# A fused attention and expert layer on one core: a new order at the step's border, and work moved from VectorE to GpSimd

## The reference

```python
q, k, v = x @ wq + bq, x @ wk + bk, x @ wv + bv        # 16 heads of 8
q, k = rope(q), rope(k)
scores = q k^T / sqrt(8), masked above the diagonal
x = layernorm(x + softmax(scores) v @ wo + bo)
probs = softmax(x @ wg)                                # 8 experts, top 1
location = number of earlier tokens (of all 16 sequences) with the same expert
keep a token if location < 512
x = layernorm(x + keep * gate * (x @ W[expert]^T + b[expert]))
```

## Time and profile before

| | |
|---|---|
| median of three runs | 492.28 us |
| the profiled execution: its time, its span | 493.83 us, 492.2 us |
| TensorE busy, weight loads busy | 85%, 74% of the span |
| VectorE, ScalarE, GpSimd busy | 70%, 34%, 34% |
| mean granted TensorE clock | 0.948 |
| instructions | 10410 |

### The profile page before, as it was taken

How to read it: one execution, slowest core, us unless ns; L and a number is a source line. 1 busy time by engine, 2 the same in 40 slices (tenths; PEclk the granted TensorE clock), 3 DMA queues, 4 the chain that set the end, 5 groups by cost and what they waited for, 6 DMA issues and landing times.

```text
span 492.2 us, 10410 instructions
## 1 busy us (share of the span) xinstructions
PE 418.6 (85%) x3270; PEld 362.4 (74%) x3270; DVE 345.4 (70%) x910; ACT 169.0 (34%) x370; POOL 165.2 (34%) x288
## 2 busy tenths in 40 slices
PE   2527398999999999999999999999999999989551
PEld 2425287979788888888888878787879787868441
DVE  7677346678787877788787878778777786844542
ACT  4404134333342424243333434333434342424100
POOL 5423202131424242433424251525252523231232
PEclk9997588999999999999999999999999999999856
DMA  4163977939385856777585849393939393310000
GB/s 119 48 102 90 150 137 107 140 87 137 74 147 86 144 79 135 91 126 97 121 104 121 106 105 126 90 135 82 149 83 140 84 141 65 30 31 1 11 1 21
DMA packets 145443, 47.29 MB, mean 96 GB/s; under 512 B 104317, under 2 KB 141697, under 8 KB 145418
## 3 DMA queue, kind: packets, MB, share of 16 engines
q1 hardware_dynamic: 141194, 43.30, 55.0%
q10 hardware_dynamic: 3456, 1.57, 1.8%
q0 software_dynamic: 768, 2.10, 1.5%
HBM read 30.70 MB, written 14.68 MB: 92 GB/s over the span
## 4 chain that ended last, share of the span: by engine, by line
PE 65%; DVE 17%; issue 6%; ACT 5%; SPq 2%; DMA 2%; POOL 1%; ACTq 1%; DVEq 0%; POOLq 0%
PE ps_pv L853 27%; PE ps_m L774 6%; PE ps_b L820 5%; PE ps_m L775 5%; PE ps_m L776 5%; DVE y_sel L616 4%; PE ps_a L830 4%; PE ps_m L794 3%; PE ps_b L805 2%; ACT probs L473 2%; PE ps_a L805 2%; PE ps_n L861 2%; DMA k_diag<-plain_parts 1%; SPq L314 1%; PE ps_n L901 1%
## 5 line engine op out<-in xcount | busy, mean ns | idle before, releaser
L853 PE MATMUL ps_pv<-probs,v_diag 128*128 128x64 f32 (+3 forms) x1024 | 191.1, 322 | 6.1 <-ACT probs L473 6.1
L853 PEld LDWEIGHTS ps_pv<-probs,v_diag 128*128 128x128 f32 x1024 | 150.3, 193 | 16.1 <-ACT probs L473 9.1
L473 ACT ACTIVATE probs<-ps_b 128x512 f32<-128x512 f32 (+1 forms) x176 | 96.9, 559 | 141.3 <-PE ps_b L805 140.5
L631 DVE TENSOR_REDUCE row_max<-ps_a 128x2 f32<-128x512 f32 (+3 forms) x176 | 109.8, 634 | 36.7 <-PE ps_a L805 36.4
L830 PE MATMUL ps_a<-k_plain,q_diag 128*128 128x64 bf16 (+3 forms) x512 | 66.3, 242 | 12.9 <-DMA q_diag<-plain_parts 7.2
L820 PE MATMUL ps_b<-q_plain,k_diag 128*128 128x64 bf16 (+3 forms) x512 | 65.9, 237 | 2.1 <-DMA k_diag<-plain_parts 2.1
L616 DVE TENSOR_REDUCE y_sel<-ps_m 128x128 f32<-128x1024 f32 x32 | 39.2, 1225 | 38.0 <-PE ps_m L794 37.3
L830 PEld LDWEIGHTS ps_a<-k_plain,q_diag 128*128 128x128 bf16 x512 | 35.3, 102 | 23.4 <-DVE row_max L631 13.0
L820 PEld LDWEIGHTS ps_b<-q_plain,k_diag 128*128 128x128 bf16 x512 | 37.6, 99 | 10.2 <-DMA k_diag<-plain_parts 2.4
L413 POOL COPY v_diag<-v_rows 64x128 f32<-64x128 f32 x64 | 18.6, 291 | 78.2 <-ACT v_rows L487 76.2
L805 PE MATMUL ps_a<-mask_a_bf,ident_bf 128*128 128x128 bf16 (+2 forms) x176 | 44.6, 253 | 0.0
(11 more groups left out here) (141 smaller groups left out, 695.9 us busy)
## 6 DMA issues: line engine op xcount, KB each, us to landing
plain_parts<-rot SPq DMA_DIRECT2D x192, 64.0 KB, 2.0
k_plain<-plain_parts SPq DMA_DIRECT2D x16, 384.0 KB, 3.8
q_diag<-plain_parts SPq DMA_DIRECT2D x32, 192.0 KB, 5.4
q_plain<-plain_parts SPq DMA_DIRECT2D x16, 384.0 KB, 6.1
k_diag<-plain_parts SPq DMA_DIRECT2D x32, 192.0 KB, 6.5
x_in<-in_L_attn_x_dram SPq DMA_DIRECT2D x16, 128.0 KB, 5.7
x_res<-in_L_attn_x_dram SPq DMA_DIRECT2D x16, 128.0 KB, 3.1
out_dram<-y_out POOLq DMA_DIRECT2D x16, 128.0 KB, 2.5
```

The source lines that it names most:

```text
L473: act.activation(probs[:, k % PR, 0:cols], ps_b[k % 2][:, 0:cols], ACT.Exp, scale=SCALE)\
L631: last = dve.tensor_reduce(row_max[:, NBLK - 1 - j, groups[0]:groups[-1] + 1], scores[:, :, col:col + width(j)], AX.X, ALU.max)
L853: mm = pe.matmul(ps_pv[:, g // 4, BLK * j:S], v_diag[q][:, j, 128 * g:128 * g + 128], probs[:, k % PR, col:col + width(j)], start=(j == 0 ...
```

## The change

- Maxima: chunks 2 to 8 stand in slots 0, 2, 3, 4, 5, 6, 7, and chunks 9 and 10 both in slot 8; slot 1 has none.
- TensorE, slot 11: the turn stands behind that slot's PV. Slot 13: the experts' second half stands behind chunk 10's PV.
- ScalarE: the weighted copies stand directly behind the sums copies in slot 13.
- VectorE: the first reciprocal is in slot 13 of the same step, the second in slot 0 of the next; the second selection moves to slot 3 of the next step, the experts' addition from slot 3 to 4; the four rotation products stand ahead of the gate and route operations; the maxima parts and the sum `rot` are no longer here.
- GpSimd: the maxima parts stand behind the `v_diag` copies; the sum `rot` stands behind `seen`.

```diff
+MAXIMA_IN = {0: (2,), 2: (3,), 3: (4,), 4: (5,), 5: (6,), 6: (7,), 7: (8,), 8: (9, 10)}
...
         def maxima_at(slot, a, b):
-            if slot < NCH - EARLY:
-                return (b, slot + EARLY) if has(b) else (None, 0)
             if slot >= SLOTS - EARLY:
-                return (a, slot - (SLOTS - EARLY)) if has(a) else (None, 0)
-            return None, 0
+                return [(a, slot - (SLOTS - EARLY))] if has(a) else []
+            return [(b, k) for k in MAXIMA_IN.get(slot, ())] if has(b) else []
...
@@ gpsimd
                     last.then_inc(s_["v_done"], 1)
                     after(pool, "v_done", b, 1, 1)
+                    after(pool, "a_taken", b, NCH, NCH)
+                    after(pool, "ex_ready", b)
+                    pool.tensor_tensor(max_wide..., row_max..., C("head_is")..., ALU.mult).then_inc(s_["widened"], 1)
+                    after(pool, "widened", b, 1, 1)
+                    pool.nop(nofuse=True)
+                    pool.tensor_copy(max_part(0), by_half(max_wide)).then_inc(s_["parted"], 1)
+                    after(pool, "parted", b, 4, 1)
+                    pool.tensor_tensor(by_half(max_rest), by_half(max_wide), max_part(0), ALU.subtract)\
+                        .then_inc(s_["parted"], 1)
+                    after(pool, "parted", b, 4, 2)
+                    pool.nop(nofuse=True)
+                    pool.tensor_copy(max_part(1), by_half(max_rest)).then_inc(s_["parted"], 1)
+                    after(pool, "parted", b, 4, 3)
+                    pool.tensor_tensor(max_part(2), by_half(max_rest), max_part(1), ALU.subtract)\
+                        .then_inc(s_["parted"], 1)
...
                 if has(n):
+                    after(pool, "roped", n, 1, 1)
+                    pool.tensor_tensor(rot[:, :, :], rot_c[:, :, :], rot_s[:, :, :], ALU.add).then_inc(s_["rot_done"], 1)
                     after(pool, "rot1_done", n, 1, 1)
...
@@ scalar
-                    if slot == 0 and has(d):
-                        copy_pairs(weighted, 0).then_inc(s_["pv_copied"], 1)
...
                         copy_pairs(sums, 1).then_inc(s_["sums_copied"], 1)
+                        copy_pairs(weighted, 0).then_inc(s_["pv_copied"], 1)
...
@@ vector
-                    if slot in (12, 13) and has(d):
-                        select(d, slot - 12)
-                    if slot in (1, 2) and has(d):
-                        after(dve, "sums_copied", d, 1, 1)
-                        half_cols = slice(128 * (slot - 1), 128 * slot)
-                        dve.reciprocal(inv_den[:, half_cols], sums[:, half_cols]).then_inc(s_["den_done"], 1)
+                    if slot == 12 and has(d):
+                        select(d, 0)
+                    if slot == 3 and has(e):
+                        select(e, 1)
+                    if slot == 13 and has(c):
+                        after(dve, "sums_copied", c, 1, 1)
+                        dve.reciprocal(inv_den[:, 0:128], sums[:, 0:128]).then_inc(s_["den_done"], 1)
+                    if slot == 0 and has(d):
+                        dve.reciprocal(inv_den[:, 128:S], sums[:, 128:S]).then_inc(s_["den_done"], 1)
...
-                    if slot == 3 and has(e):
+                    if slot == 4 and has(e):
                         add_experts(e)
...
-                    if slot == 9 and has(b):
...
+                    if slot == 10 and has(n):
+                        after(dve, "qk_ready", n, 1, 1)
+                        after(dve, "rot_done", n)
+                        for i in range(2):
...
+                        last.then_inc(s_["roped"], 1)
                     if slot == 10 and has(d):
                         after(dve, "egate_done", d, 1, 1)
...
-                    if slot == 10 and has(n):
...
-                        dve.tensor_tensor(rot[:, :, :], rot_c[:, :, :], rot_s[:, :, :], ALU.add).then_inc(s_["rot_done"], 1)
...
             all_steps(dve, step)
+            select(B - 1, 1)
             add_experts(B - 1)
...
@@ tensor
-                    if slot == 13 and has(d):
-                        experts(d, n, 1)
-                    if slot == 11 and has(b):
-                        after(pe, "parted", b, 4, 4)
...
                     k = slot - PV_SLOT
                     if has(c) and 0 <= k < NCH:
...
+                    if slot == 11 and has(b):
+                        after(pe, "parted", b, 4, 4)
...
+                    if slot == 13 and has(d):
+                        experts(d, n, 1)
```

More of the change, by code:

```diff
@@ L621, in step @@
                 for slot in range(SLOTS):
-                    t, k = maxima_at(slot, a, b)
-                    if t is not None:
+                    for t, k in maxima_at(slot, a, b):
                         after(dve, "a_ready", t, NCH, k + 1)
@@ L725, in step @@
                         dve.tensor_tensor(gate_kept[:, :], n_kept[:, :], gate[:, :], ALU.mult).then_inc(s_["gk_done"], 1)
-                    if slot == 10 and has(n):
-                        after(dve, "qk_ready", n, 1, 1)
-                        for i in range(2):
-                            dve.scalar_tensor_tensor(out=rot_c[:, i, :], in0=ps_m[:, 0, S * i:S * i + S],
-                                                     scalar=bias_cols[:, 2 * i:2 * i + 1], in1=C("cos"),
-                                                     op0=ALU.add, op1=ALU.mult)
-                            last = dve.scalar_tensor_tensor(out=rot_s[:, i, :], in0=ps_m[:, 1, S * i:S * i + S],
-                                                            scalar=bias_cols[:, 2 * i + 1:2 * i + 2], in1=C("sin"),
-                                                            op0=ALU.add, op1=ALU.mult)
-                        last.then_inc(s_["roped"], 1)
-                        after(dve, "roped", n, 1, 1)
-                        after(dve, "rot3_done", n)
-                        dve.tensor_tensor(rot[:, :, :], rot_c[:, :, :], rot_s[:, :, :], ALU.add).then_inc(s_["rot_done"], 1)
                     if slot == 10 and is_step(s, -2):
@@ L832, in step @@
                         masks(ps_a[k % 2], CHUNKS[k], mask_a_bf, True).then_inc(s_["a_ready"], 1)
-                    if slot == 13 and has(d):
-                        experts(d, n, 1)
-                    if slot == 11 and has(b):
-                        after(pe, "parted", b, 4, 4)
-                        if has(d):
-                            after(pe, "route_done", d, 1, 1)
-                        for i in range(NBLK // 2):
-                            mm = pe.matmul(ps_n[:, BLK * i:BLK * i + BLK],
-                                           max_parts[:, 2 * i:2 * i + 2, :].rearrange("p i m -> p (i m)"), stacked_bf[:, :],
-                                           start=(i == 0), stop=True, skip_group_check=True)
-                        mm.then_inc(s_["ex_ready"], 1)
                     if slot == 12 and has(d):
@@ L856, in step @@
                         mm.then_inc(s_["pv_ready"], 1)
+                    if slot == 11 and has(b):
+                        after(pe, "parted", b, 4, 4)
+                        if has(d):
+                            after(pe, "route_done", d, 1, 1)
+                        for i in range(NBLK // 2):
+                            mm = pe.matmul(ps_n[:, BLK * i:BLK * i + BLK],
+                                           max_parts[:, 2 * i:2 * i + 2, :].rearrange("p i m -> p (i m)"), stacked_bf[:, :],
+                                           start=(i == 0), stop=True, skip_group_check=True)
+                        mm.then_inc(s_["ex_ready"], 1)
+                    if slot == 13 and has(d):
+                        experts(d, n, 1)
                     if slot == 4 and has(d):
```

27 lines of the change are left out of this document (11 added, 16 removed).

## The result

| | before | after |
|---|---|---|
| median of four runs each, same chip | 491.78 us (489.36 to 495.66) | 469.92 us (469.69 to 471.06) |
| ratio | | 0.9553, 95% interval 0.9488 to 0.9618 |
| profiled execution: time, span | 493.83, 492.2 us | 469.89, 468.2 us |
| TensorE, VectorE, GpSimd busy | 85%, 70%, 34% | 87%, 68%, 44% |
| mean granted TensorE clock | 0.948 | 0.948 |

The forecast was 473 us (466 to 485), faster. Taken apart by chunk 0's exponential in each step, the 24.0 us between the two spans lie here (before, after, in us). The profiled execution of before stands 2.05 us over its median and that of after at its median, so about 2 us of the 24.0 belong to that one execution, and one profile can't say to which row of the table.

A forecast was written before the change was run, and what follows sets the result against it. TensorE's waits at three places were taken as the bound. Gains 1.1 + 0.3 less 0.1 and 0.1 made a 24.4 us step, -15.6 over thirteen; with the ends -19.2, so 473 us (8 in 10: 466 to 485).

The forecast's parts named there:

- The border, 1.1 us: From chunk 10's PV and the experts' second half to chunk 0's PV: 5.2 us instead of 6.3, gain 1.1 per step.
- VectorE behind the border, 0.1 charged: VectorE's maxima of chunks 2 to 8 end just in time for TensorE; 0.1 us per step charged for slots 8 and 9.
- Chunk 10's PV, 0.1 charged: TensorE reaches this PV about when ScalarE's exponential for it ends, 4.0 us after the turn; 0.1 us charged.
- The turn, 0.3 us: TensorE's wait for `kept` in a full step shrinks from 0.55 to 0.25 us, gain 0.3.
- The parts on GpSimd, 2 us: The five maxima operations take about 2 us on GpSimd (bounds 1.5 and 6.5), ready a little over 1 us early, costing nothing.
- The start, +0.65: Chain to the first `ps_b` scores: sequence 1's slower `rot` sum +0.47 and hand-over 0.2, together +0.65 us.
- Sequence 0's step, +0.5: No experts' second half there and the turn one PV later: between 0 and +1.0, taken as +0.5 us.
- The last two steps, -4.7: Step 16: -1.7 us for covered copies, -1.0 for the clock; step 17: -2.0 for earlier reciprocals.
- VectorE the bound: Rival: reciprocals, attn and second selection among the maxima make TensorE wait 0.8 us more per step, 483 to 485; chance 0.15.
- All waits go: Rival: the small charged waits are pipelined away too, so 466 us; chance 0.07.
- GpSimd and VectorE hold each other: Rival: freed 2.2 us return as longer operations on both, full steps gain nothing, only the ends: 489 us; chance 0.07.
- A late turn: Rival: GpSimd's parts at 1.16 us each put the turn some 3 us late, step 27.4, 512 us; chance 0.09.

The follow-up runs named there:

- experiment 2: The kernel before with only the new border (TensorE order, ScalarE's copies, selections, reciprocals, experts' sum): 490.79 us, ratio 0.9992.
- experiment 4: The kernel before with the new border and the new maxima table; maxima parts, sum and products stay on VectorE in old order: 475.78 us, ratio 0.9689.
- experiment 1: The changed kernel with the old border (experts' second half ahead of chunk 10's PV; copies, selections and reciprocals back): 487.65 us, ratio 0.9905.
- 9: The changed kernel with one unused 128x512 operation more on GpSimd in each step, ahead of the maxima parts: 472.64 us, ratio 0.9625.
- 10: The changed kernel with three unused 128x512 operations more on GpSimd in each step, ahead of the maxima parts: 497.96 us, ratio 1.0162.
- 7: The changed kernel with the sum `rot` of every sequence on VectorE, right behind the products: 477.52 us, ratio 0.9763.
- 3: The changed kernel with the old maxima table, one chunk in each slot 0 to 8 except two as before: 485.31 us, ratio 0.9855.
- 5: The changed kernel with the turn ahead of slot 11's PV, as before: 481.04 us, ratio 0.9774.
- experiment 8: The changed kernel with the five operations of the maxima parts back on VectorE, ahead of the logits: 476.02 us, ratio 0.9675.
- 6: The changed kernel with VectorE's four rotation products behind gate and `kept`, as before: 476.51 us, ratio 0.9690.
- experiment 11: The changed kernel with GpSimd's late memsets begun only after VectorE's late casts: 467.12 us, ratio 0.9483.
- 12: The changed kernel with GpSimd's late memsets behind VectorE's late casts, and `rot` of sequences 0 and 1 on VectorE: 464.78 us, ratio 0.9484.

## Why the prediction held, and where its sizes were off

**What bounds it** was right: the time lay in TensorE's waits at three places, and it is TensorE with hardly a wait now.

**The border, 1.1 us**: right in size, wrong in what it hangs on. The working named "one maximum's scores" ahead of the mask, and "three more groups in between", without saying that the table makes it so. Experiments 2 and 4: the border without the table gives a full step nothing (25.69), with it 0.89, and taking either out of the changed kernel costs the same (25.27 and 25.26). The table alone on the kernel before was not run; experiment 1 has it without the border, and there it and all the rest give 0.34. It is one step made of two edits.

**VectorE behind the border, 0.1 charged**: the reading of VectorE was right. Chunks 2 to 8 were to run from u = 2.45 to 11.65 and ran from 2.43 to 11.48. (The old stretch that it was read from holds seven maxima, as the new one does, and not six.) The one wait that was counted in the border, chunk 4's scores for chunk 2's maximum, is there: they start 0.18 us behind the mask ahead of them, where a group that waits for nothing starts 0.06 behind. The 0.1 charged for what comes after is not there.

**Chunk 10's PV, 0.1 charged**: it is there. It starts 0.15 to 0.36 us behind the mask ahead of it, in the mean 0.23, where other PVs start 0.06 behind, so it costs 0.17.

The step is 24.2 instead of 24.4, and 13 x 0.2 = 2.6 us of the 3.1 by which the steps' gain was under-forecast. Of the 0.2, 0.1 is the wait that is not there and 0.1 the turn (next paragraph), less 0.07 for chunk 10's PV; which row holds the small rest is open.

**The turn, 0.3 us**: right, if a little small (0.67 to 0.30 between starts in the mean, 0.4 once the 0.06 and 0.11 that such starts are apart without a wait are taken off), and it takes all of the other four edits. Undone one at a time they cost 0.88, 0.48, 0.74 and 0.29 us, far more together than their joint gain over experiment 4, 24.72 - 24.22 = 0.50: with the turn late and the products early, `kept` comes just in time, and whatever is put back ahead of it is waited for.

**The parts on GpSimd, 2 us**: five operations from 269.21 to 271.03, 1.82 us, near the value taken and far from 6.5. They are ready 1.9 us ahead of the turn, where a little over 1 was forecast. The margin is bounded by experiments 9 and 10: one operation more costs a full step nothing, three cost 1.75.

**The sum on GpSimd "costs nothing in a full step"**: right as a cost, though it takes 1.30 us and not 1.16. That leaving it on VectorE would cost 0.74 was not in the prediction.

**The start, +0.65**: 2.3. The term itself was right. From x's low part to ScalarE's first cast of `rot` it is 32.49 to 38.98 = 6.49 us, before 31.04 to 36.90 = 5.86: +0.63. What it left out is 0.24 us behind it, in the writes and reads, and 1.45 us ahead of it: x's low part at 32.49 instead of 31.04, behind VectorE's casts that GpSimd's memsets hold.

Of these 1.45 us, 0.13 stand already at sequence 0's low part. The rest can be taken apart, because ten other profiles have the same code there but for the place of the sum. From sequence 0's low part to the next it is 18.67 us (before, experiment 2) or 19.35 (experiments 4 and 7) with the sum on VectorE, and 19.3 (3, 5, 8), 19.7 (10) or 20.0 (changed kernel, 1, 6, 9) with it on GpSimd. Which of its levels a profile shows is chance, by which cast slips in between two memsets: the identity cast took 2.61 or 5.29 us in the first group, 0.28, 3.25 or 5.9 in the second. That is 0.68 us of the difference. But both levels stand 0.64 us later with the sum on GpSimd: sequence 0's sum runs there too, and so GpSimd's memsets start at 22.81 instead of 22.04. So 0.64 us are a cost of the change, and the failed step is that I priced the start for sequence 1's sum alone, on one profiled execution, and not for what sequence 0's sum pushes back on GpSimd.

**Sequence 0's step, +0.5**: 1.0, but not for the reason given. The wait of chunk 10's PV grew, from 1.48 to 2.04; yet counted from sequence 0's exponential this PV starts at 19.23 us where it started at 19.87. The clock rose sooner on the way there (0.94 in the mean instead of 0.88), so what the later turn cost can't be read apart from it. From the PV to sequence 1's exponential it is 5.30 us instead of 3.62, at a mean clock of 0.50 instead of 0.80. First row the wait, second the window behind it:

```profile
81.70 0.69 PE L842 MATMUL ps_pv<-probs,v_diag 128*128 128x64 f32 x2 [2.04 <-ACT probs L493]
```

```profile
81.70:84.00 2.30, 2.30 (x11) 2.30 (x12) 0.00 (x0) 0.00 (x0) 2.09 (x3) 0.50 0.33 85
```

The granted clock is 0.50 there (1.2 GHz), and PV starts come 0.21 us apart; before, behind 1.48 us, they came 0.11 apart at 1.00 (2.4 GHz), and the clock fell only behind that PV (0.54 from 82 to 84 us). So the term that the sum put at nothing here is the clock.

**The last two steps, -4.7**: -8.6. The wait of 1.73 us became 0.41, the one for attn 3.21 became 1.31, both as forecast. Missed were, first, the waits that before had in the step ahead (0.54 for the expert choice, 0.34 at the turn, 0.43 for the first selection, all gone: TensorE is busy for all of the 21.27 us); in experiment 8 that interval is 0.9 us longer again. Second, the clock: from attn to the end the mean is 0.66 where it was 0.57, and that stretch is 26.5 us instead of 28.2. This second part is not the change's alone: with the same work behind the last exponential 0, experiments 9, 11 and 12 took 48.3 to 48.4 us for it, where the changed kernel's profile has 46.12.

**The rivals.** *VectorE the bound*: refuted, the one maximum for which TensorE waits costs 0.1 us. *All waits go*: the step of 24.2 lies between its 23.9 and the forecast's 24.4, and 469.92 us lie about as far from the forecast's 473 as from this rival's time (its sum is 25.6 us and not 26, so 467); 0.5 us of waits are left in a step (0.13 for the maximum, 0.19 at the turn, 0.17 for chunk 10's exponential). *GpSimd and VectorE hold each other*: no in the full steps, yes at the start. In a full step GpSimd's sum (272.36 to 273.66) stretches `gate_kept` from 0.16 to 0.65 us, and a filler the expert choice; for neither does TensorE wait longer. *A late turn*: the mechanism is real but needs three fillers.

```profile
273.03 0.65 DVE L739 TENSOR_TENSOR gate_kept<-n_kept,gate 128x2 f32<-128x2 f32 x1
```

The Trainium skill (GPSIMD Engine Reference, Key points) says which VectorE instructions collide with GpSimd: those in a two-port mode or with two SBUF inputs. This case's traces agree for the full steps: the two-input `gate_kept` and `chosen` were held, and beside the same filler the one-input `first` kept its 0.17 us. The casts that were held at the start have one input; whether they ran in a two-port mode, no row shows.

## What to carry to other kernels

Edits that each remove one of several waits in a row must be costed as a group: the border without the table gave a full step nothing, and with it 0.9 us. Before giving an operation to another engine, look at everything the receiving engine already does beside the giving one, the start included, and not at the moved operation alone. And where an engine waits at one point for the later of two chains, an order that costs nothing is the one that puts both just ahead of their own consumer: here products before gate, turn behind one more PV.

## What the hardware showed unasked

GpSimd can hold one VectorE cast across several of its own operations: 5.92 us for a cast that takes 0.25 us alone, across five memsets and to the end of the last. With the memsets put behind the casts the hold was gone (experiment 11). In other profiles the same cast got in between two memsets. A two-input GpSimd operation does it too. VectorE and GpSimd with one filler:

```profile
269.67 0.17 DVE L710 TENSOR_REDUCE first<-rank 128x2 f32<-128x16 f32 x1
...
269.87 0.95 DVE L713 TENSOR_TENSOR chosen<-rank,first 128x16 bf16<-128x16 f32 x1
```

```profile
269.48 1.31 POOL L418 TENSOR_TENSOR fill<-cst 128x512 f32<-128x512 f32 x1
```

The choice ends at 270.82, as the filler does (270.79). And on operations this small GpSimd is hardly slower than VectorE: the five of the maxima parts took 1.82 us together against 1.58 on VectorE in the kernel before (274.12 to 275.70), though one operation on 128x512 takes 1.30 us against 0.69. The parts were a good choice for GpSimd; the sum only because nothing waits for it there.
